# Attention rows transposed ahead of the k product and split a turn sooner, slots ahead of the second y tile

## What is computed

```
q, k, v = x @ w_q.T, x @ w_k.T, x @ w_v.T          # 16 heads of 16
attn    = softmax(q k.T / 4) v                     # per sequence and head
x1      = layernorm(x + attn @ w_o.T)
gates   = softmax(x1 @ gating_w); the 2 best of 8 experts, with capacity 1280
out     = layernorm(x1 + sum of the chosen experts' relu(x1 @ w1 + b1) @ w2 + b2, weighted)
```

## Time and profile before

| what | us |
|---|---|
| median of 3 runs | 813.63 |
| lowest, highest | 812.87, 816.58 |
| the profiled execution's own time | 811.73 |
| its span, first to last instruction | 810.0 |
| x transposes of sequence 5 to those of sequence 15 | 77.44 to 259.99 |
| x transposes of sequence 12 to those of sequence 13 (one full round of 8 turns) | 205.23 to 223.49 |

### The profile page before, as it was taken

One profiled execution on the slowest core, in us unless ns is written; L12 is line 12 of the kernel. 1 busy time (PEld: TensorE's weight loads), 2 busy tenths in 40 slices (PEclk: granted clock), 3 DMA queues, 4 the chain that ended last, 5 costly groups with the idle time before them and its releaser, 6 DMA issues.

```text
span 810.0 us, 17161 instructions
## 1 busy us (share of the span) xinstructions
PE 770.3 (95%) x5919; PEld 641.9 (79%) x5919; DVE 595.3 (73%) x1309; ACT 446.3 (55%) x881; POOL 417.0 (51%) x643
## 2 busy tenths in 40 slices
PE   7699999999999998989999999999999999999993
PEld 7577777777777755878888888988988988988993
DVE  6767888888888998958568568568557566575982
ACT  3177777777777777535345435435344443444770
POOL 1001266666556667664463462552552653637774
PEclk9789999999999999999999999999999999999997
DMA  5577776454666473362452452451532533524841
GB/s 158 135 172 164 159 162 157 121 122 121 134 142 125 107 185 92 97 180 38 98 111 40 91 113 38 97 112 31 145 60 73 110 52 79 110 47 69 322 163 49
DMA packets 71537, 92.78 MB, mean 115 GB/s; under 512 B 12972, under 2 KB 55885, under 8 KB 71324
## 3 DMA queue, kind: packets, MB, share of 16 engines
q1 hardware_dynamic: 53308, 67.95, 31.7%
q0 software_dynamic: 16928, 22.15, 15.8%
q10 hardware_dynamic: 1216, 1.57, 0.9%
HBM read 39.18 MB, written 26.89 MB: 82 GB/s over the span
## 4 chain that ended last, share of the span: by engine, by line
PE 81%; DVE 8%; DMA 4%; issue 3%; POOL 3%; ACT 0%; POOLq 0%; DVEq 0%; SPq 0%
PE wide L1731 9%; PE wide L1733 9%; PE wide L1732 9%; PE bank L1764 8%; PE halves_wide L1764 8%; PE bank L993 6%; PE halves_wide L993 6%; PE wide L1025 5%; DVE negm L903 4%; PE halves_wide L1766 4%; PE bank L1766 4%; PE bank L1107 4%; PE wide L1032 2%; PE halves_wide L1140 2%; DMA rows<-x_rows,lists 1%
## 5 line engine op out<-in xcount | busy, mean ns | idle before, releaser
L1405 POOL DMA_INDIRECT acc_rows<-o_w,lists x70 | 120.9, 1728 | 174.6 <-ACT o_w L1554 160.9
L903 DVE TENSOR_REDUCE negm<-wide 128x2 f32<-128x512 f32 x256 | 163.8, 684 | 38.7 <-PE wide L1025 37.0
L1521 ACT ACTIVATE h<-wide,b1T 128x512 f32<-128x512 f32 (+1 forms) x200 | 115.4, 601 | 91.1 <-PE wide L1733 69.1
L656 ACT ACTIVATE probs<-wide 128x512 f32<-128x512 f32 x256 | 139.1, 598 | 39.4 <-PE wide L1032 37.5
L1731 PE MATMUL wide<-g_hi,stack 128*128 128x512 f32 (+1 forms) x400 | 139.7, 349 | 1.8 <-ACT h L1521 1.1
L1733 PE MATMUL wide<-g_hi,stack 128*128 128x512 f32 (+1 forms) x400 | 139.3, 348 | 0.0
L1732 PE MATMUL wide<-g_lo,stack 128*128 128x512 f32 (+1 forms) x400 | 139.2, 348 | 0.0
L1554 ACT ACTIVATE o_w<-o_b,lists 128x256 f32<-128x256 f32 x70 | 35.7, 510 | 147.9 <-DVE o_b L1692 147.9
L1025 PE MATMUL wide<-stack 48*128 48x256 f32 x512 | 94.5, 312 | 7.0 <-DVE negm L903 6.2
L1025 PEld LDWEIGHTS wide<-stack 48*128 48x128 f32 x512 | 67.7, 190 | 41.2 <-issue 20.3
L1394 POOL DMA_INDIRECT rows<-x_rows,lists x80 | 84.1, 1051 | 30.8 <-issue 23.8
(11 more groups left out here) (237 smaller groups left out, 1812.8 us busy)
## 6 DMA issues: line engine op xcount, KB each, us to landing
stack<-qk SPq DMA_DIRECT2D x180, 128.0 KB, 3.9
w_raw<-in_L_ffn_w SPq DMA_DIRECT2D x16, 1024.0 KB, 5.9
x_sb<-in_L_attn_x SPq DMA_DIRECT2D x16, 256.0 KB, 4.9
x_rows<-x SPq DMA_DIRECT2D x16, 256.0 KB, 3.7
acc_rows<-x SPq DMA_DIRECT2D x16, 256.0 KB, 4.5
acc_sb<-acc_rows SPq DMA_DIRECT2D x8, 512.0 KB, 8.7
out<-acc_sb SPq DMA_DIRECT2D x8, 512.0 KB, 2.7
x_rows<-zrow SPq DMA_DIRECT2D x2, 1152.0 KB, 7.0
```

The source lines that it names most:

```text
L656: nc.scalar.activation(probs[:, i % 4, x].rearrange("p c t -> p (c t)"), shifted_banks(i)[:, x, :], ACT.Exp, scale=SCALE).then_inc(exp_don ...
L903: nc.vector.tensor_reduce(negm[n % 2][:, :, x, u], score_banks(PAIRS * n + u)[:, x, :].rearrange("p (c t) -> p c t", c=QC), X, ALU.max, ne ...
L1405: nc.gpsimd.indirect_dma_start(out=acc_d, out_offset=bass.IndirectOffsetOnAxis(ap=lists[:, e, QC * c + r, 0:1], axis=0), in_=o_w[c][:, r, ...
L1521: ins = nc.scalar.activation(h[u % 2][:, t], banks[BZ[u % 4]][:, t], ACT.Relu, bias=b1T[:, FT * e + f:FT * e + f + 1])
```

## The change

Three blocks change place; nothing is added or removed.

- TensorE, turn 4: the four `attn` transposes stand ahead of the k product, not behind it.
- ScalarE, turn 4: `aT_hi` stands ahead of the k copy, right behind `mT_hi`, and VectorE: `aT_lo` is issued at the end of turn 4, behind `mT_lo`, not in turn 5 behind the reductions.
- VectorE, turn 7: `slots(m)` stands ahead of the second y tile.

```diff
@@ scalar_program, behind mT_hi
+                m = due(turn, AT, NB)
+                if m is not None:
+                    act.wait_ge(aT_ready, m + 1)
+                    act.wait_ge(o_ready, QC * m)
+                    nc.scalar.activation(aT_hi[:, :, :], bank(BA, a=DK), ACT.Copy).then_inc(aT_hi_done, 1)
@@ scalar_program, behind the k copy
-                (the same five lines)
@@ vector_program, behind the reductions
-                m = due(turn, AT + 1, NB)
-                if m is not None:
-                    dve.wait_ge(aT_hi_done, m + 1)
-                    nc.vector.tensor_tensor(aT_lo[:, :, :], bank(BA, a=DK), aT_hi[:, :, :].bitcast(F32),
-                                            ALU.subtract).then_inc(aT_lo_done, 1)
...
+                m = routed(turn, SLOT)
+                if m is not None:
+                    slots(m)
                 m = due(turn, O + 1, NB)
                 if m is not None:
                     rows_out(m, 1)
-                m = routed(turn, SLOT)
-                if m is not None:
-                    slots(m)
@@ vector_program, behind mT_lo
+                m = due(turn, AT, NB)
+                if m is not None:
+                    dve.wait_ge(aT_hi_done, m + 1)
+                    nc.vector.tensor_tensor(aT_lo[:, :, :], bank(BA, a=DK), aT_hi[:, :, :].bitcast(F32),
+                                            ALU.subtract).then_inc(aT_lo_done, 1)
@@ tensor_program, behind the x transposes, ahead of the q and k products
+                m = due(turn, AT, NB)
+                if m is not None:
+                    pe.wait_ge(attn_done, m + 1)
+                    transpose4(BA, attn, (1, 0)).then_inc(aT_ready, 1)
@@ tensor_program, behind the k product
-                (the same four lines)
```

More of the change, by code:

```diff
@@ L702, in scalar_program @@
                     x_hi(1)
-                m = due(turn, AT, NB)
-                if m is not None:
-                    act.wait_ge(aT_ready, m + 1)
-                    act.wait_ge(o_ready, QC * m)
-                    nc.scalar.activation(aT_hi[:, :, :], bank(BA, a=DK), ACT.Copy).then_inc(aT_hi_done, 1)
                 m = due(turn, PV0 + 2, NB)
@@ L1168, in tensor_program @@
                     by_feature_tile(k_bank(n), 1, n).then_inc(k_ready, 1)
[L1169 to L1172, removed]
                 if turn == K + 1:
```

## The result

The changed kernel takes 807.79 us (median of 14 runs, 805.77 to 811.15), the kernel before 812.08 (14 runs, 809.73 to 816.58): a ratio of 0.9948, 95% interval 0.9936 to 0.996, or 4.2 us less. A second series of runs gave 0.996 (0.9947 to 0.9973), with medians of 808.11 and 812.15. The forecast was 810.3 us with a range from 807.9, so the time lies 0.1 us outside; the interval of the ratio, 806.9 to 808.8 us, has that bound inside it. The profiled execution has a span of 805.9 us, where it was 810.0.

A forecast was written before the change was run, and what follows sets the result against it. TensorE was taken to bound attention, with only two recurring waits to win. Terms -2.9 - 1.56 + 0.6 + 0.53 gave -3.3 us, from a median of 813.63 to 810.3 us; 8-in-10 range 807.9 to 813.4.

The forecast's parts named there:

- the bound: Ten rounds of attention: TensorE busy 179.29 of 182.55 us, so only its recurring waits can be won.
- both waits: TensorE: x transposes waiting for slots, 2.9 us over ten rounds; output product waiting for `aT_lo`, 1.6 us over twelve.
- the 0.03 given back behind the x transposes: TensorE, turn 7: transposes pass faster after a wait, so removing 0.32 us of slot wait gains 0.29 a round.
- the margin of the slots: VectorE, turn 7: slots finish 0.41 us sooner against transposes 0.33 late, so the wait goes with 0.08 us spare.
- `aT_hi`'s end: ScalarE, turn 4: `aT_hi` done at about 216.24 us, early enough for `aT_lo` to fit with 0.3 us spare.
- the loss in sequence 12: Sequence 12's turn 4, without a k product: later VectorE reductions delay the output product, losing 0.53 us once.
- the slower rival: VectorE, end of turn 4: late `aT_hi` makes `aT_lo` delay turn 5's reductions; +5.9 us, 819.5 us, chance 0.05.
- rival E: TensorE, turn 4: six transposes in a row drop the clock in twelve k products; +13.5 us, 827.1 us, chance 0.02.
- the order on TensorE (turn 4): `attn` transposes ahead of the k product lengthen turn 4 from 2.19 to 2.24 us, losing 0.6 us over twelve rounds.
- rival A: TensorE in attention: as forecast, both recurring waits go; 810.3 us, chance 0.58.
- rival C: Attention and tail: more gained, tail loss absorbed, new order not slower, small delays end; -4.7 us, 808.9 us, chance 0.13.
- the sum of -3.3: Whole kernel: two waits gained, less the turn 4 order and sequence 12 losses: -2.9 - 1.56 + 0.6 + 0.53 us.

## Why the prediction was wrong

These steps of the prediction were right: the bound (TensorE and only its two recurring waits), both waits gone in full (-0.32 us and -0.13 a round in means over nine rounds), the 0.03 given back behind the x transposes (0.383 to 0.412), the margin of the slots (0.08 worked out, 0.08 to 0.09 read), `aT_hi`'s end (1.83 us behind the maxima's transposes worked out, 1.75 read), the loss in sequence 12 (0.53 worked out, 0.57 and 0.59 read), and roughly the price of the slower rival.

On the clock: six transposes in a row now stand ahead of the k product, and it runs at the full granted clock, 1.00, 2.4 GHz:

```profile
213.69:215.29 1.60, 1.60 (x15) 1.46 (x13) 1.60 (x4) 1.18 (x3) 0.84 (x4) 1.00 0.00 0
```

The Trainium skill, "TensorE: Matmul & The Clock Gate", section "Part 4: PE-mode transpose", says that the clock does not come up for transposes. The drop that the prediction drew from it as rival E did not happen. Whether transposes alone would bring the clock up, which is what the sentence is about, no run here shows.

The step that failed is "the order on TensorE (turn 4)", a term of the sum that was mis-sized. It took 0.41 us from `attn` transposes to k product from the x transposes and the v product; the runs show 0.355 in all six kernels that have this order, while x transposes to v stay at 0.41 wherever they do not wait. Turn 4 is not 0.05 longer but 0.015 shorter (2.177 against 2.192, means over nine rounds and both traces): 12 x 0.065 = 0.8 us, and with it the sum is -4.1 us. The -0.015 is inside the bounds given for the term (-0.05 to +0.1 a round), so the mechanism, rival A, held, together with the part of rival C by which the new order is not slower. A round takes 17.81 us, not 17.88. Measured is -4.2 us in the first series (0.9948 of 812.08); in the second it is -4.0 by the medians and -3.2 by the ratio (0.996).

The traces also show where the 0.055 us lies, and it is not at the product. Read one by one, the four x transposes start 0.165, 0.109 and 0.109 us apart, and the v product 0.028 after the last; the four `attn` transposes of turn 4 start 0.109 apart all three times, and the k product the same 0.028 after the last. Only the first step differs, and it goes by what stands in front. It is 0.165 where transposes without a wait follow scores: so for x, for u with the 128x256 q product behind them, and for the `attn` rows of sequence 14, the one place where these follow scores. It is 0.109 for `attn` behind the k product or behind the maxima's transposes. Where transposes had to wait first, it lies between 0.135 and 0.167. Sequence 14 in the kernel before, and the same step in the other ten traces is 0.163 to 0.165:

```profile
314.03 0.50 PE L1032 MATMUL wide<-stack 50*128 50x256 f32 x4
314.46 0.66 PE L1002 MATMUL halves_wide<-ident,attn 128*128 128x128 f32 x4
```

So four take 0.66 us there and behind the scores of the earlier trace rows, and 0.60 in the earlier trace rows: the rows on which the prediction was worked out had the difference already. Why the first step behind scores is longer, no run tells.

The larger part of the distance between 810.3 and 807.79 us is the level that the forecast was counted from: the three runs shown had a median of 813.63, the fourteen 812.08, which is 1.6 of the 2.5 us. From there even the sum of -3.3 gives 808.8 us, and from 813.63 the sum of -4.1 gives 809.5: either alone is inside the range, both together put the time 0.1 us outside it, which is less than the runs can tell apart.

Open is the handover, in which the changed kernel's two traces lose up to 1.1 us less to the wait for gathered rows than the others do. The list load ahead of it landed sooner, but the kernel with sequence 12 left alone issues the same work and does not show it, and over the whole stretch from sequence 15 on the spread of one and the same code, 0.7 to 0.8 us, leaves little of it. It was not in the forecast with either sign.

## What to carry to other kernels

On a saturated engine, price a wait by start-to-start distances against the same pair of neighbours elsewhere without the wait, and for a new order take rows with the same neighbour in front: four transposes cost 0.06 us more behind scores than behind other transposes. When a producer's step is moved on one engine, move it in every in-order queue on its way: TensorE's part alone cost 0.33%, VectorE's alone 1.07%; all three together took 1.48 us off ten rounds, and with the slots the kernel gained 0.5%. Filling idle time is free only where that idle time is: the same edit lost 0.6 us up to the output product of the one sequence that had no cover.

## What was not expected of the hardware

The first 60 us, which no edit touches, end between 59.6 and 61.7 us over eleven traces, 2.1 and 1.1 us apart in the two kernels that were traced twice. That is as large as half of the effect studied, so a difference of spans between two single traces says little, while a stretch inside a trace repeats to 0.05 us once a single late DMA is taken out.
